# Split-precision projections, three value buffers and a shifted store written by the layer norms, in a macaron transformer kernel

## The reference, cut to what matters

```python
x = x + 0.5 * experts(layernorm(x))          # 8 experts
x = x + linear_attention(layernorm(x))
x = x + 0.5 * experts(layernorm(x))
x = x + 0.5 * local(layernorm(x))            # 6 layers
x = x + full_attention(layernorm(x))
x = x + 0.5 * local(layernorm(x))            # 6 layers, same weights

def local(x):                                # for each of 6 layers
    x = attn_layer(shift_tokens(x), ...) + x
    x = ffn_layer(shift_tokens(x), ...) + x
def attn_layer(x, Wqkv, qs, ks, Wo):
    q, k, v = split(x @ Wqkv, 3, -1)         # 128 -> 3 x 1024, 16 heads of 64
    q, k = l2norm(q) * qs, l2norm(k) * ks    # then rotary with a scale
    # windows of 32 tokens: each query sees its own window and the one before
    return local_attention(q, k, v) @ Wo
```

## Time and profile before

| | before |
|---|---|
| median of 3 runs | 4659.25 us |
| the profiled execution's own time | 4663.63 us |
| its span, first to last instruction | 4661.8 us |
| mean granted TensorE clock | 0.961 |
| busy share: TensorE / its weight load / VectorE / ScalarE / GpSimd | 93% / 61% / 74% / 53% / 51% |
| DMA queue of SyncE | 246.30 MB, 19.7% of 16 engines |

### The profile page before, as it was taken

The page is one execution under the profiler, slowest core; times in us unless marked ns, Lnnn a source line. Parts: engine busy times, 40 slices in busy tenths (PEclk is TensorE's granted clock), DMA queues, the critical chain, the costliest instruction groups (busy, mean ns, idle before and its releaser), DMA issues. The chain is left out here.

```text
span 4661.8 us, 152491 instructions
## 1 busy us (share of the span) xinstructions
PE 4330.6 (93%) x67144; PEld 2856.8 (61%) x67144; DVE 3453.7 (74%) x4473; ACT 2462.5 (53%) x2820; POOL 2390.8 (51%) x3067
## 2 busy tenths in 40 slices
PE   8999988999999999999968898799999999999997
PEld 5666665666666666666643332566666666666664
DVE  3333348888888888888848885788888888888885
ACT  1121114665665665666626776356666656566654
POOL 0000007666666666666614342466666666666663
PEclk8988989999999999999978998899999999999999
DMA  1000012222322222222200000223222232222221
GB/s 61 9 9 10 18 40 67 64 77 68 79 63 76 67 68 78 66 76 72 75 4 1 1 1 1 74 63 80 68 77 63 67 82 64 74 73 73 66 68 51
DMA packets 150985, 255.71 MB, mean 55 GB/s; under 512 B 37320, under 2 KB 41040, under 8 KB 150224
## 3 DMA queue, kind: packets, MB, share of 16 engines
q1 hardware_dynamic: 150352, 246.30, 19.7%
HBM read 50.09 MB, written 1.05 MB: 11 GB/s over the span
## 5 line engine op out<-in xcount | busy, mean ns | idle before, releaser
L608 PE MATMUL psum<-loc_wqkv,loc_zs 128*128 128x512 f32 x2304 | 1120.4, 610 | 20.9 <-DVE loc_zs L1157 15.7
L608 PEld LDWEIGHTS psum<-loc_wqkv,loc_zs 128*128 128x128 f32 x2304 | 404.6, 192 | 373.9 <-issue 331.1
L963 POOL TENSOR_TENSOR loc_rc_k<-loc_rc_k,loc_rs_k 128x1024 f32<-128x1024 f32 x192 | 454.5, 2367 | 149.1 <-DVE loc_rs_k L1044 148.8
L703 PEld LDWEIGHTS psum<-loc_PT,loc_V 64*64 64x64 f32 x24576 | 392.9, 135 | 195.6 <-issue 194.6
L703 PE MATMUL psum<-loc_PT,loc_V 64*64 64x32 f32 x24576 | 422.8, 220 | 48.9 <-issue 42.6
L963 POOL TENSOR_TENSOR loc_rc_q<-loc_rc_q,loc_rs_q 128x1024 f32<-128x1024 f32 x192 | 453.1, 2360 | 0.0
L841 ACT ACTIVATE loc_sq_k<-psum 128x1024 f32<-128x1024 f32 x192 | 196.6, 1024 | 482.8 <-PE psum L608 482.8
L722 PEld LDWEIGHTS psum<-loc_outT,loc_wo 128*128 128x128 f32 x3072 | 377.9, 194 | 98.2 <-issue 93.1
L938 POOL TENSOR_TENSOR loc_rt<-loc_rn 128x32 f32<-128x32 f32 x192 | 45.8, 238 | 691.3 <-DVE loc_rn L1040 686.8
L722 PE MATMUL psum<-loc_outT,loc_wo 128*128 128x128 f32 x3072 | 378.9, 277 | 2.0 <-DVE loc_gg L1100 1.9
L969 POOL TENSOR_TENSOR loc_qk_q<-loc_rc_q,loc_rn 128x1024 f32<-128x1024 f32 x192 | 365.5, 1904 | 26.7 <-issue 0.4
(11 more groups left out here) (178 smaller groups left out, 9013.6 us busy)
## 6 DMA issues: line engine op xcount, KB each, us to landing
loc_V<-loc_V SPq DMA_DIRECT2D x1152, 128.0 KB, 2.3
loc_V<-loc_V SPq DMA_DIRECT2D x672, 64.0 KB, 2.0
loc_wqkv<-in_wqkv SPq DMA_DIRECT2D x42, 512.0 KB, 3.9
moe_w<-in_moe_w SPq DMA_DIRECT2D x32, 256.0 KB, 3.5
loc_wo<-in_wo SPq DMA_DIRECT2D x12, 512.0 KB, 4.5
loc_w<-in_w SPq DMA_DIRECT2D x12, 341.0 KB, 3.2
loc_w<-in_w SPq DMA_DIRECT2D x12, 192.0 KB, 3.1
loc_scales<-in_scales SPq DMA_DIRECT2D x14, 128.0 KB, 3.5
```

The lines of the kernel that those rows point to most:

```text
L608: mm = pe.matmul(M.bank[bank + g], zs[:, s, i * P:(i + 1) * P], wqkv[:, k, g * T:(g + 1) * T], start=True, stop=True)
L703: mm = pe.matmul(M.bank[WB + c][64 * j:64 * j + 64, m * P + q:m * P + q + 32], V2[r:r + 64, i, w, p * 64:(p + 1) * 64], PT[r:r + 64, p, q: ...
L963: pool.tensor_tensor(rc[:, :], rc[:, :], rs[:, :], ALU.add).then_inc(added, 1)
```

## The change

The layer norms ahead of the local blocks write their last product straight into the shifted store `M.zs` (two operations of 64 partitions for one of 128), and `zs`, its memset and its two copies go out of the block. The block now keeps each weight matrix and the tokens as a pair of float32r tiles: VectorE masks the low 12 bits (`cut_*`), ScalarE copies the masked value into the high tile (`round_*`), GpSimd subtracts it from the original into the low tile (`rest_of_*`). Weights are cut per layer and matrix, tokens per sequence, four steps ahead. A projection is three products per 512 columns. `V` and `V2` have three buffers in rotation, one squares tile serves q and k, and the full attention block's weights are loaded when that block starts.

```diff
-                dve.tensor_tensor(dst[:, s * T:(s + 1) * T], dst[:, s * T:(s + 1) * T], RSTD[s % 2][:, :],
-                                  ALU.mult).then_inc(out_ready, 1)
+                if shifted is None:
...
+                else:
+                    dve.tensor_tensor(shifted[0:64, s, 0:T], dst[0:64, s * T:(s + 1) * T], RSTD[s % 2][0:64, :], ALU.mult)
+                    dve.tensor_tensor(shifted[64:P, s, 1:T + 1], dst[64:P, s * T:(s + 1) * T], RSTD[s % 2][64:P, :],
+                                      ALU.mult).then_inc(out_ready, 1)
...
+    KEPT = 3
+    SLOT = {1: 0, 2: 1, 0: 2}
...
             def load_qkv(L, k, loaded):
-                sp.dma_start(wqkv[:, k, :], W["wqkv"][ds(L, 1), :, k * INNER:(k + 1) * INNER]
+                m = 3 * L + SLOT[k]
+                if m >= 2:
+                    sp.wait_ge(w_split, m - 1)
+                    sp.sem_inc(sp_passed, 1)
+                sp.dma_start(wraw[:, m % 2, :], W["wqkv"][ds(L, 1), :, k * INNER:(k + 1) * INNER]
...
-                if n == TS - 1 and live(n):
-                    sp.wait_ge(k_full, upto(L, TS - 1))
-                    sp.sem_inc(sp_passed, 1)
-                    load_qkv(L + 1, 1, wk_loaded)
...
+                if n == TS - 1 and L + 1 < DEPTH:
                     load_qkv(L + 1, 0, wq_loaded)
                 load_values(L, n)
+                if n == 3 and L + 1 < DEPTH:
+                    load_qkv(L + 1, 1, wk_loaded)
+                    load_qkv(L + 1, 2, wv_loaded)
...
                 for g in range(2):
-                    mm = pe.matmul(M.bank[bank + g], zs[:, s, i * P:(i + 1) * P], wqkv[:, k, g * T:(g + 1) * T],
-                                   start=True, stop=True)
+                    cols = slice(g * T, (g + 1) * T)
+                    pe.matmul(M.bank[bank + g], z_lo[:, r, tokens], w_hi[:, k, cols], start=True, stop=False)
+                    pe.matmul(M.bank[bank + g], z_hi[:, r, tokens], w_lo[:, k, cols], start=False, stop=False)
+                    mm = pe.matmul(M.bank[bank + g], z_hi[:, r, tokens], w_hi[:, k, cols], start=False, stop=True)
...
             def project_q(L, t, full):
                 if t == 0:
-                    pe.wait_ge(wq_loaded, L * 16 + 16)
+                    pe.wait_ge(w_high, 3 * L + 3)
+                    pe.wait_ge(w_split, 3 * L + 3)
...
+            def round_weights(L, k):
+                act.wait_ge(w_cut, 3 * L + SLOT[k] + 1)
+                act.wait_ge(q_full if k == 0 else k_full if k == 1 else v_full, upto(L, -1))
+                act.activation(w_hi[:, k, :], w_bits[:, :], ACT.Copy).then_inc(w_high, 1)
...
             def copy_v(L, t):
                 act.wait_ge(v_full, upto(L, t))
+                before = t - 2 if t >= 2 else t - 2 + TS
+                if L or t >= 2:
+                    act.wait_ge(v2_loaded[before % TILES], v2_count(L if t >= 2 else L - 1, before))
...
                 if live(n - 3):
                     copy_out(L, n - 3)
+                if n == 0 and 0 < L < DEPTH:
+                    round_weights(L, 0)
+                if n == TS - 1 and L + 1 < DEPTH:
+                    round_weights(L + 1, 1)
                 if live(n - 2):
                     exponential(L, n - 2)
...
                     copy_v(L, n)
+                    if n == TS - 1 and L + 1 < DEPTH:
+                        round_weights(L + 1, 2)
                     square_q(L, n)
...
+            def rest_of_weights(L, k):
+                m = 3 * L + SLOT[k]
+                pool.wait_ge(w_cut, m + 1)
+                pool.wait_ge(q_full if k == 0 else k_full if k == 1 else v_full, upto(L, -1))
+                pool.tensor_tensor(w_lo[:, k, :], wraw[:, m % 2, :], w_bits[:, :], ALU.subtract).then_inc(w_split, 1)
...
+                if n == 0 and 0 < L < DEPTH:
+                    rest_of_weights(L, 0)
                 if live(n):
                     total_of(L, n, k_rotated, rc_k, rs_k, k_added)
-
+                if n == TS - 1 and L + 1 < DEPTH:
+                    rest_of_weights(L + 1, 1)
+                    rest_of_weights(L + 1, 2)
+                if n % TILES == 2 and L < DEPTH:
+                    after, s = divmod(n // TILES + 1, SEQS)
+                    if L + after < DEPTH:
+                        rest_of_tokens(L + after, s)
...
+            def cut_weights(L, k, loaded):
+                m = 3 * L + SLOT[k]
+                dve.wait_ge(loaded, L * 16 + 16)
+                if m:
+                    dve.wait_ge(w_high, m)
+                    dve.wait_ge(w_split, m)
+                dve.tensor_scalar(w_bits[:, :].bitcast(I32), wraw[:, m % 2, :].bitcast(I32), LOW_BITS, None,
+                                  ALU.bitwise_and).then_inc(w_cut, 1)
...
                     by_sine(L, n, 3, X_, rs_k, k_rotated)
+                if n == TS - 1 and L + 1 < DEPTH:
+                    cut_weights(L + 1, 1, wk_loaded)
+                if n == 0 and 0 < L < DEPTH:
+                    cut_weights(L, 0, wq_loaded)
...
                     normalise(L, n - 2)
+                if n == TS - 1 and L + 1 < DEPTH:
+                    cut_weights(L + 1, 2, wv_loaded)
                 if live(n):
                     by_cosine(L, n, 0, q_squared, W_, rc_q, q_ready)
...
-            dve.memset(zs[:, :, :], 0.0).then_inc(cleared, 1)
-            dve.wait_ge(cleared, 4)
-            x_in = M.xh[:, :].rearrange("p (s n) -> p s n", n=T)
-            dve.tensor_copy(zs[0:64, :, 0:T], x_in[0:64])
-            dve.tensor_copy(zs[64:P, :, 1:T + 1], x_in[64:P]).then_inc(zs_ready, 1)
+            cut_tokens(0, 0)
+            cut_weights(0, 1, wk_loaded)
+            cut_weights(0, 2, wv_loaded)
+            cut_weights(0, 0, wq_loaded)
```

174 lines of the change are left out of this document (115 added, 59 removed).

## The result

Measured: **4798.57 us** (median of 4 runs, 4793.5 to 4808.76) against 4659.37 for the kernel before on the same chip: ratio 1.0298, 95% interval 1.0271 to 1.0324. The forecast was 4645 us with a range up to 4712, so it missed by 154 us.

A forecast was written before the change was run, and what follows sets the result against it. TensorE and a VectorE-GpSimd loop of 15.6 us per tile were taken to bound the kernel. 4663.6 - 100 (projections) + 78 (boundaries) + 8 (starts) = 4649.6; the same step from 4659.25 gave 4645, own range 4625 to 4665, overall 4590 to 4712.

The forecast's parts named there:

- Projections: TensorE: six float32r products at 0.215 us take 1.29 against 1.72, saving 0.43 per projection, at most 248 us.
- Rival C: TensorE projections: float32r loads not hidden or 128 rows cost more, six products 1.92 us, 4860 us in all; chance 0.05.
- What the floor leaves: Ordinary steps: VectorE and GpSimd's loop holds 15.6 us per tile, so only 100 us of the projection saving counts.
- classes 1 to 3: Steps by tile number n mod 4, cosine k to cosine k: forecast to shorten by 1.25, 0.35 and 0.95 us.
- instruction supply: TensorE's instruction-fetch gaps: 0.15 us allowed in steps with n mod 4 = 3.
- Weight splitting: Layer boundaries, steps 15 and 0: cuts and roundings delay the exponential and cosine q; 7.8 us each, 78 for ten.
- Step 15: A layer's last step, to the next layer's first cosine k: 26.1 us against 21.6, 4.5 more.
- GpSimd has room: Step 15: GpSimd's weight subtractions, 2.4 us each for k and v, end at 13.75, with the root at 16.5.
- rival D: Boundary weight cuts: VectorE and GpSimd block each other, 30 cuts waiting 2.36 us each, 71 us, 4716; chance 0.08.
- rival B: Steps 15 and 0: ScalarE's rounding queue holds back an exponential; 14 us per boundary with low clock, 4707 us; chance 0.22.
- Token splitting, three buffers, one squares tile: Ordinary steps: cuts fit in existing gaps, copies and squares wait for nothing new; cost nothing.
- Starts: Block starts, layer norms and the full block's weight load: 5 + 1.4 + 2 = 8 us more in all.

The follow-up runs named there:

- e17: e4 plus three one-column bfloat16 products ahead of each tile's mask products and 12 tiny products at the first local block's start: 4632.0 us, ratio 0.9936.
- e18: e17 with 23 instead of 12 tiny products at the first local block's start, so every 256th record falls 44 records later: 4718.9 us, ratio 1.0129.
- e3: The changed kernel with the old float32 projections and nothing split; the new storage, norms and full-block loads remain: 4652.4 us, ratio 1.0002.
- e2: e1 with tokens split only for the first two sequences, so no step holds splitting; three products remain: 4672.1 us, ratio 1.0047.
- e4: e2 with only the high times high product of the three: 4663.1 us, ratio 1.0019.
- e6: The kernel before with three feed-forward pieces ahead of the values on TensorE and VectorE's attention addition behind the normalising: 4694.5 us, ratio 1.0073.
- e7: e2 with the same new order of TensorE and VectorE as e6: 4717.9 us, ratio 1.0130.
- e5: The changed kernel with ScalarE's key and value weight rounding behind its query and key copies, query weights' behind the value copy, two bit buffers: 4790.5 us, ratio 1.0265.
- e13: The changed kernel with e5's later rounding and without GpSimd's weight subtractions after layer 0: 4754.6 us, ratio 1.0215.
- e10: e5 with the query weights cut ahead of the rotation factors and rounded right behind the exponential: 4766.5 us, ratio 1.0237.
- e1: The changed kernel with weights split for layer 0 only and used in all six layers; tokens still split: 4669.0 us, ratio 1.0048.
- e11: The kernel before with GpSimd's reciprocal root leaving out its second refinement: 4629.0 us, ratio 0.9944.
- e12: e2 with GpSimd's reciprocal root leaving out its second refinement: 4612.9 us, ratio 0.9894.

## Why the prediction was wrong, step by step

- **Projections: mis-sized, right kind.** Float32r does stream once and the full-array loads do run under the matmuls, all but a little: the products start 0.232 us apart, not 0.215, so a projection is 1.39 us and saves 0.33, not 0.43. Rival C is out. By the rule of the Trainium skill's "TensorE: Matmul & The Clock Gate" (Part 3, The mechanism), that a weight load overlaps a running matmul only where the row groups differ, six products would have been 1.92 us (an estimate); the trace disagrees again.
- **What the floor leaves: this step failed.** It counted 92 us of gain in classes 1 to 3 (100 with the first layers). The levels that it forecast, 16.65, 16.25 and 17.35 us, were not far off: in steps with neither a pause nor a stretch of low clock class 1 went from 17.5 to 17.1, class 2 from 16.2 to 16.3, class 3 from 17.9 to 17.3, and in e17, with far shorter projections, class 1 is 16.7. (The recorded terms of class 3 add up to 16.9, not 17.2.) But these levels were held against means before (17.9, 16.6, 18.3) that have pauses and low clock in them. Of the 92 us some 30 were a gain of such undisturbed steps; 18 were a level of class 1 set too low; the other 44 were disturbances of the kernel before, which the step let vanish without a reason. They did not vanish: the means after stand some 90 us above the undisturbed steps, 18.0, 16.6 and 18.7. The undisturbed steps after are few (5 to 16 per class, by how short a pause still counts), and their means move by 0.2 us with that choice, so these parts are rough.
- **The term that was nearly missing: instruction supply.** I allowed 0.15 us in class 3 for it. The pauses went from 91 to 158 us, and between e17 and e18 146 us of such pauses, with the clock behind them, cost 87. They go with the work between scores and values: with 1.72 us of projection there (before, e3) they are 91 and 83, with 1.39 (e2) 140, with 0.46 (e4) 160, though e4 has the fewest records; with more work there (e6, e7) they fell. That the shorter stretch is the cause fits all of these, but the phase drifts through each of them and was not held. The clock added to it: TensorE was at the lower level for 116 and 143 us of the two blocks against 31 and 27, which is the 0.97 and 0.96 of the windows against 0.99. How much of the loss is the clock's alone wasn't separated.
- **What holds an undisturbed step** stays open. Its waits (e4) run from sine q, which frees the values' bank, through the values and a feed-forward product back to VectorE; but e6, which took those products off that path, was no faster. Several loops of nearly equal length are the likeliest reading.
- **Weight splitting: mechanism right, price too small.** Cosine q came at 13.3 (forecast 13.55). Step 15 was forecast at 26.1 and is 28.1, step 0 at 17.9 and is 19.8: 10.5 us against 7.8. Steps 1 to 3 behind it cost another 2.4 us per boundary, on which the forecast had nothing: 128 us in all, not 78. In the timeline `rescale` waits for TensorE until 25.1 us into the step instead of 23.1, because the spread product ahead of it comes late. "GpSimd has room" was wrong in a way that its own finishing times hid: e5 shows VectorE slowed beside its subtractions once ScalarE's wait is gone, and e13 that both had to go. This is rival D's mechanism behind rival B's. In e5 `normalise` took 2.91 us against 1.23 and ended 1.08 us after the subtraction beside it; the factors took up to 5.86 us in e5 and 7.44 in e10 against 1.43 at best. The Trainium skill's "SBUF — State Buffer", section "SBUF: two separate sides", has the two engines block each other on a shared port for a whole operation; by that rule, the traces agree here.
- **Token splitting, three buffers, one squares tile: right.** e2 against e1, and e3.
- **Starts: 20 us, not 8, of which the splitting shows for about half.** From the layer norm's last product to the first cosine k it is 5.4 and 5.3 us more per block than before. The rest lies ahead of it, in stretches that vary as much where nothing was changed: in e6 and e11, whose code there is that of the kernel before, the stretch ahead of the first block is 700.7 and 692.8 us against 691.7, and the one between the blocks 634.2 and 626.4 against 628.7.
- **Sum.** Steps 15 and 0 +104 instead of +78; ordinary steps +21 instead of -100 (steps 1 to 3 +24, all others -3); starts +20 instead of +8: 145 us in the profiled executions, as measured. The chance of 0.33 for slower and the 4707 of rival B were nearest, and its 14 us per boundary are near the 12.8 measured; the range failed because every rival but C kept the 100 us of gain.

What is left of the weight splitting in e13 is 75 us between the blocks of its profiled execution and e1's: 42 in steps 15 and 0, 28 in steps 1 to 3 behind them, 5 elsewhere. Which of the cuts (two of 1.0 us on average in step 15), the late query weights and the clock holds them stays open. Every version that was faster than the kernel before (e11, e12, e17) leaves out part of its computation.

## What to carry to other kernels

Before crediting an engine with a saving, ask for each step what it waits for when that work is gone: a piece counts in full only if it stands on the chain between two engines, whatever the busy shares say. Compare like with like: a floor read from undisturbed steps may not be set against a mean that has disturbances in it. Two stalls in one place hide each other, so take them away together before calling either cheap, and price a stall with the steps behind it. And look at where "issue" idle falls: where tiny instructions are dense, their number and their place in the stream are a cost of their own.

## What was not expected of the hardware

- Instructions came in packets of 16 KB, one for 256 records of TensorE (that they are TensorE's is inferred). Where such a border fell late in the dense stretch of scores and values (records 6 ns apart on average), TensorE often stood until 1.4 us after the landing of the next packet, with up to 2.9 us from one record to the next in the kernel after. The next packet started in the median 1.3 us after a border was passed and took 1.1 us.
- Shifting this border by 44 records, with equal work, moved the kernel by 87 us.
- The four factor products of VectorE took between 1.43 and 7.44 us, by what GpSimd did beside them.
- With less to do, TensorE was granted less clock: in 960 to 2300 0.99 before, 0.97 with three shorter products (e2), 0.94 with one (e4). It was 0.97 with one product and fewer pauses (e17), so the pauses have their part in it.
